# Query and key pieces laid in blocks of 16 partitions instead of every sixth partition, in a four-layer cross-attention kernel

## The reference, cut to what matters

```
scores = einsum('bqhd,bkhd->bhqk', Q, K) * scale     # 16 heads, head width 16
attn   = softmax(scores, axis=-1)                    # masked in three of the five
out    = einsum('bhqk,bkhd->bqhd', attn, V)
```

## Time and profile before

| what | value |
|---|---|
| median of 3 runs | 3543.7 us |
| lowest, highest | 3536.8, 3561.54 us |
| the profiled execution's own time | 3543.7 us |
| its span in the profile | 3541.9 us |
| PE, VectorE, ScalarE, GpSimd busy | 79%, 46%, 34%, 16% of the span |
| mean granted clock of TensorE | 0.913 |
| one round of the loop | about 430 us |

### The profile page before, as it was taken

How to read it: one execution, slowest core, us unless ns; L and a number is a source line. 1 busy time by engine, 2 the same in 40 slices (tenths; PEclk the granted TensorE clock), 3 DMA queues, 4 the chain that set the end, 5 groups by cost and what they waited for, 6 DMA issues and landing times.

```text
span 3541.9 us, 54252 instructions
## 1 busy us (share of the span) xinstructions
PE 2815.6 (79%) x18992; PEld 1925.3 (54%) x18992; DVE 1622.9 (46%) x2848; ACT 1194.2 (34%) x1830; POOL 572.2 (16%) x1308
## 2 busy tenths in 40 slices
PE   5788788877787877878778877788788887878777
PEld 3565555555555555555555555555555555646455
DVE  3544535444445444444444444444444444444453
ACT  1233333333333333333333333333333233333334
POOL 3110121111211021111111112110121101211012
PEclk9899899998999989999889999899888998899999
DMA  5110121111211112111121111211112111121112
GB/s 188 37 37 26 37 66 45 31 29 28 70 40 36 33 34 65 35 36 29 49 55 34 32 33 44 59 43 29 28 40 66 35 29 37 31 68 34 29 37 61
DMA packets 161209, 157.33 MB, mean 44 GB/s; under 512 B 17782, under 2 KB 160294, under 8 KB 160422
## 3 DMA queue, kind: packets, MB, share of 16 engines
q1 hardware_dynamic: 160934, 153.64, 15.5%
HBM read 30.20 MB, written 4.19 MB: 10 GB/s over the span
## 4 chain that ended last, share of the span: by engine, by line
PE 51%; DVE 17%; issue 10%; ACT 6%; DVEq 5%; POOL 3%; SPq 3%; POOLq 2%; DMA 2%; ACTq 0%
PE work L1069 13%; PE work L1060 10%; DVE neg_max L914 8%; PE out L1141 6%; PE unit L1097 5%; PE unit L1117 5%; PE unit L1113 4%; ACT probs L770 3%; PE unit L1094 3%; PE work L1052 3%; POOL rstd L644 2%; DVEq L930 2%; SPq L544 2%; DVE hidden_t L932 2%; DVEq L900 2%
## 5 line engine op out<-in xcount | busy, mean ns | idle before, releaser
L914 DVE TENSOR_REDUCE neg_max<-unit 128x4 f32<-128x1024 f32 x648 | 772.6, 1218 | 631.6 <-PE unit L1097 620.0
L770 ACT ACTIVATE probs<-unit 128x1024 f32<-128x1024 f32 x648 | 638.8, 1023 | 493.6 <-PE unit L1117 491.8
L1097 PE MATMUL unit<-key_stack,query_stack 96*128 96x256 bf16 x2592 | 493.3, 296 | 70.9 <-DVE neg_max L914 35.6
L1117 PE MATMUL unit<-query_stack,key_stack 99*128 99x256 bf16 x2592 | 471.8, 286 | 44.1 <-DMA query_stack<-max_rows 28.3
L1069 PE MATMUL work<-par,hidden_t 128*128 128x256 f32 x1792 | 463.9, 413 | 46.1 <-ACT hidden_t L731 27.0
L1069 PEld LDWEIGHTS work<-par,hidden_t 128*128 128x128 f32 x1792 | 359.6, 207 | 122.3 <-ACT hidden_t L731 37.9
L1097 PEld LDWEIGHTS unit<-key_stack,query_stack 96*128 96x128 bf16 x2592 | 263.8, 106 | 253.9 <-issue 75.0
L1060 PE MATMUL work<-tok_t,par 128*128 128x256 f32 x1408 | 365.3, 413 | 24.0 <-ACT tok_t L731 18.2
L1117 PEld LDWEIGHTS unit<-query_stack,key_stack 99*128 99x128 bf16 x2592 | 250.5, 102 | 137.4 <-ACT probs L770 33.5
L1060 PEld LDWEIGHTS work<-tok_t,par 128*128 128x128 f32 x1408 | 281.9, 208 | 76.4 <-ACT tok_t L731 26.2
L1141 PE MATMUL out<-probs,values 128*32 128x256 f32 x4160 | 287.1, 397 | 19.2 <-ACT probs L770 19.0
(11 more groups left out here) (146 smaller groups left out, 3383.7 us busy)
## 6 DMA issues: line engine op xcount, KB each, us to landing
query_stack<-query_pieces SPq DMA_DIRECT2D x492, 128.0 KB, 2.5
key_stack<-key_pieces SPq DMA_DIRECT2D x396, 128.0 KB, 2.4
par<-in_params SPq DMA_DIRECT2D x3, 2445.5 KB, 16.2
x_in<-in_x SPq DMA_DIRECT2D x19, 256.0 KB, 2.8
m_self<-in_mask_self SPq DMA_DIRECT2D x19, 256.0 KB, 3.2
m_cross<-in_mask_cross SPq DMA_DIRECT2D x19, 256.0 KB, 4.6
c_in<-in_ctx SPq DMA_DIRECT2D x18, 256.0 KB, 2.7
out<-result SPq DMA_DIRECT2D x16, 256.0 KB, 2.2
```

The lines of the kernel that those rows point to most:

```text
L770: a_.activation(probs[:, n % PROB_BUFS], bank[:], ACT.Exp, scale=SCALE[l]).then_inc(exped, 1)
L914: v.tensor_reduce(neg_max[:, u // 4, :, 2 * (u % 4):2 * (u % 4) + 2], bank[:], AX.X, ALU.max, negate=True).then_inc(maxed, 1)
L1097: last = pe.matmul(bank[:, t, i, :], query_stack[s][0:ROWS, h, t * P:(t + 1) * P], key_stack[s][0:ROWS, 0 if l == "l2" else h, :], start=m ...
L1117: last = pe.matmul(bank[:, k, i, :], key_stack[s][0:MAX_ROWS, 0 if l == "l2" else h, k * P:(k + 1) * P], query_stack[s][0:MAX_ROWS, h, :], ...
```

## The change

The destination of each piece DMA becomes a block of 16 adjacent partitions: set `at` lies on partitions `16*at` to `16*at + 15`. Queries and keys are laid the same way, so each row of a matmul's contraction still meets its partner, and the 96 rows are the same rows in another order. The rows of the maxima stay on partitions 96 to 98. No instruction is added, removed or moved on any engine; number, size and source of the DMAs, and the waits, stay as they are.

```diff
@@ -536,7 +536,7 @@
                         for at, which in enumerate(rows):
                             if which != piece:
                                 continue
-                            dst = stack_[at:ROWS:len(rows), :, :]
+                            dst = stack_[HD * at:HD * (at + 1), :, :]
                             if keys and l == "l2":
                                 sp.dma_start(dst[:, 0, :], pieces[0:HD, piece, 0, :]).then_inc(placed, 16)
                             else:
```

## The result

The changed kernel takes 3803.7 us (median of four runs, 3793.1 to 3826.4), the kernel before 3546.1 us beside it: a ratio of 1.072, 95% interval 1.068 to 1.075. The forecast was 3710. The sign came as predicted, and so did the mechanism up to the landing of a batch. The time lies inside the range of 3560 to 3810, but close to its upper end: the loss is 257 us where 164 to 167 were worked out.

The account below looks back on a forecast made before the run. PE, busy 79% of the span, and its waits for batches were taken as the bound. Delays of 24.0 us a round, times 0.85 over eight rounds, plus 4 us before the loop, gave 167 us more: 3710, range 3560 to 3810.

Parts of the forecast that it names:

- A set and a batch: Piece DMAs: a set's move takes 1.1 us instead of 0.65, a batch of six lands after 8.3 us, 2.7 later.
- the 12 KB row on three partitions: Trace of the kernel before: 12 KB on three neighbouring partitions landed after 2.19 us, 0.49 more than 8 KB spread.
- the middle between 0.85 and 1.3: Move of one 128 KB piece DMA onto neighbours: 0.85 us at least, 1.3 at most, 1.1 taken.
- 1.7 + 6 x 1.1: Landing of a six-DMA batch: 1.7 us for a small DMA plus six queued moves of 1.1 us, 8.3 us.
- The places: Waits at max0 and one turn DMA per round where later landings delay PE: together 24.0 us a round.
- "issue" waits: PE's idle time ahead of max0 in the l steps, read as waiting for the query batch, 5.7 us after first issue.
- The 0.85: Factor on the 24.0 us a round for waits absorbed elsewhere and TensorE cooling: 20.4 us a round, 163 in eight.
- The range: Whole kernel: 3560 to 3810 us, said to hold about 8 in 10; the forecast's own ends were 3600 and 3805.
- spread doesn't matter: Rival on the piece DMAs: engines write at their own pace wherever the bytes go; 3544 us, chance 0.13.
- neighbours are faster: Rival on the piece DMAs: neighbours are written without mutual wait, landing 0.16 us sooner; 3536 us, chance 0.02.
- only the last move shows: Rival on the batches: moves overlap, 0.45 us more at six max0 and one turn; 3565 us, chance 0.13.
- The choking queue: Rival on the DMA queue: moves near 1.3 us, SP's issues stretch, cover is lost, nothing absorbed; 3850 us, chance 0.12.

Follow-up runs that it names:

- the later layouts: Query and key sets on every second partition (0.9999) or every third (1.008, 3591.4 us), both against the kernel before.
- keys alone: Only the key sets lie in blocks of 16 partitions, queries on every sixth as in the kernel before: 1.005 of its time, 3583.0 us.
- fillers: Constant matmuls put ahead of max0's wait in seven places of the changed kernel, none in self of stream 1: 3756.2 us, 1.054 of the kernel before.
- fillers in eight places: Changed kernel with constant matmuls ahead of max0's wait, 42 of them in self of stream 1: 3812.7 us, 1.073 of the kernel before.

## Why the prediction was right in kind and a third too small

**A set and a batch: right.** 1.1 us for a move was forecast, and 1.06 between landings was measured. A batch was to last 8.3 us and its median is 8.49 (before 6.06; the quiet ones went from 5.6 to 8.4). The value came out of the 12 KB row on three partitions, and the later layouts show why that row was the right one to ask: it was the only one of before with neighbours in it. That the middle between 0.85 and 1.3 was right is luck, since no row chose it. And the working `1.7 + 6 x 1.1` holds only as a sum. The first set of a batch now lands after 3.3 us instead of 2.3, a rise of 1.0 where the forecast had 0.45; sets in a row then follow each other more closely than they take alone. In the kernel before, sets in a row landed 0.66 us apart, which is the pace of SP's issue (0.64), so the 0.65 us of a move was an upper bound there. 120 GB/s were expected in a window over a batch and 110 stood there.

**The places: right in sum, mixed in detail.** PE's stands, medians over the rounds of the two traces, in us:

```text
place                before  after  more  forecast
l1 of stream 0         0.5    3.4    2.9    2.7
l1 of stream 1         1.9    4.8    2.9    2.7
l2 of stream 1         1.4    3.3    1.9    2.7
l3 of stream 0         0.0    1.7    1.7    2.7
l3 of stream 1         1.8    4.1    2.3    2.7
self of stream 1       5.4   10.9    5.5    3.7
self of stream 0       0.0    1.9    1.9    2.1
cross of stream 1      0.4    1.9    1.5    2.0
cross of stream 0      0.0    0.0    0.0    0.3
turn in l1, stream 1   0.5    2.9    2.4    2.4
sum                                 23.0   24.0
```

Too little was given to `self` of stream 1, whose query batch now lands 13.5 us after its first issue (before 8.1), and too much to `l3` of stream 0 and `l2` of stream 1, where PE had some room. PE starts 0.1 to 0.3 us after the last landing in all the places that the prediction counted as tight, so it read the "issue" waits rightly; in `self` of stream 1 it did not see that the first 3.0 of the 5.4 us are the rest of the loop's branch, in which PE could have done nothing else. That the keys of the other attentions cost nothing held as well: keys alone 0.5%.

**The 0.85: the step that failed.** The prediction let two effects cancel in one factor: other waits absorb some of the stand, and a longer stand cools TensorE. It forecast 167 us of more standing, and PE's idle time grew by 165.3. So as a factor on idle time 0.85 was about right (165.3 of 8 x 23.0 = 184 us). As a factor on the whole loss, which it was meant to be, it was wrong: the span grew by 251.8 us, 1.37 times the sum of the places. For cooling lengthens PE's work, not its standing, and so needed a term of its own, and that term is 86.5 us, 10.8 a round. With this measured term the sum is 3541.9 + 167 + 86 = 3795 of span, beside the 3793.7 of the profile. The prediction put the cost of PE's matmuls at nothing, and expected them to keep their durations, because the instructions stay the same; its own remark on the cooling spoke against that. The row was at hand: 0.78 behind the 5.08 us stand, and 0.61 us for a mask matmul that takes 0.38. What was left out was to multiply it by the number of places where a stand would now be nearly as long as that one. The two effects are not independent either. Work at the slower clock leaves the other engines time to catch up, and where fillers kept the clock up, idle time and filler came to 26 us more (one profile each).

**The range: kept by luck.** Its upper end stood for a move of 1.3 us, which by the forecast's own sum gives 3805. The measured 3803.7 comes from a move of 1.06 us and a slower PE. The range held, but not for the reason that it was built on.

**The rivals.** That spread doesn't matter (3544) and that neighbours are faster (3536) fell with the first landing row. That only the last move shows (3565) fell with the batch, 2.4 us longer rather than 0.45. The choking queue (3850) is the nearest in time, but not in mechanism: a move takes 1.06 us and not 1.3, SP's issue is 602 ns in the median, and its stretches (4.75 us in `self`, where before had 5.35) are no longer. Its "nothing is absorbed" describes the total no better, since the excess lies in PE's work.

## What to carry to other kernels

It pays to look at which partitions a DMA into SBUF writes when they are few. Here, with 16 partitions of 8 KB each, every second was as good as every sixth, and sixteen neighbours cost 0.4 us more per 128 KB in a row of such DMAs and 1.0 us more for the first. Where several of them stand in one line ahead of a wait, that becomes 2.4 us a batch, and two slow batches in a line cost more than twice one. When PE's stands grow, two terms belong in the sum: the idle time, and PE's own work at the lower clock behind each longer stand, which here was half the size of the first. And before a stand is filled with other work, it pays to see what it consists of: at the top of a loop a part of it can be the branch.

## What was not expected of the hardware

- The clock's share: 18992 unchanged matmuls took 2815.6, 2902.1 and, with fillers in eight places, 2810.5 us.
- PE's branch back to the top of the loop took 4.1 us in the kernel before and 7.7 in the changed one, where the piece DMAs beside it are slower, and 8.4 where both batches go ahead of the loads. VectorE's branch in the same loop took 0.07 us.
- Partitions 32 apart share a way into SBUF, as the four layouts together tell: with sets at every third partition a landing took 2.9 us, at every second 2.4.
- A 12 KB DMA that followed such a batch landed after 4.64 us, before 2.19: small transfers pay for the layout of large ones ahead of them.
